# Preparation of an adaLN block on one core: four buffers of normalised tokens, modulation rows as two lines spread by transfers, values of nine tiles ahead of the scores

## The chip, the cores and the metric

The kernel runs on one core of a Trainium2 chip. The metric is the device time of one execution in microseconds (us); a kernel is given by the median of its runs.

## The reference

Two batches of 2048 tokens of width 256. Six modulation vectors come from `silu(c) @ wmod`. Then

```python
h = layernorm(x) * (1 + ca) + sa
q, k, v = h @ Wq, h @ Wk, h @ Wv            # 16 heads, key width 16, value width 64
attn = softmax(q k / 4, over the query axis)
x = x + ga * (attn @ v) @ Wo
h = layernorm(x) * (1 + cb) + sb
x = x + gb * ffn(h)     # gate, up (704 wide) and down, all with blockwise FP4 quantisation
```

`ga` and `gb` are pushed away from zero: `(2 * (g >= 0) - 1) * max(|g|, 0.25)`. All is float32.

## The kernel before

The program is written out by hand: five functions, one for each engine (`tensor_program`, `scalar_program`, `vector_program`, `gpsimd_program`, `sync_program`), each a fixed order of instructions, joined by semaphores. In the text PE is TensorE, DVE is VectorE, ACT is ScalarE, POOL is GpSimd, SP is SyncE, whose queue issues nearly all transfers. A float32 product is made of three products of 'high' and 'low' parts (`products`, L397), so most operands stand in two tensors, `*_hi` and `*_lo`.

For each batch `b` there is a preparation and then an attention loop; after both batches follows the feed-forward part (32 token tiles).

**Preparation** (`prepare_pe`, `prepare_act`, `prepare_dve`, `prepare_pool`). The tokens are 16 tiles of 128, in four groups `g` of four tiles. For a group DVE takes mean and variance (`stats`, L849), POOL the inverse root (`inverse_root`, L1162), DVE normalises (`normalise`, L859) into the buffer `xn_r`, which holds two groups, PE transposes (`turn_tokens`, L403), ACT applies the modulation and writes `hT` and its high part (`take_tokens`, L678), DVE makes the low part (`low_tokens`, L870). Then PE makes queries and keys of the group in four pieces `r` of six matmuls each (`queries_keys`, L446), ACT and DVE write the two halves of each piece (`part_act`, L691; `part_dve`, L942) and SP stores them to DRAM (L354). PE waits for `tok_low` before each group. When all 16 pieces have landed, SP loads them for heads 0 and 1 as stacks `stq`, `stk` (`load_stack`, L297, 8 transfers a head); later heads are loaded during the loop.

Then come the values (`values`, L453): for each of `EARLY` tiles PE makes two halves of 512 columns, six matmuls each; ACT copies the first (L709), DVE the second (L955). The results stand in four PSUM quarters used in rotation; the table `bank_uses` says who used a quarter before, and `take_quarter` waits until that one was read. In batch 0 the modulation rows stand behind tile 3 (`mod_rows_pe`, L460; `mod_rows_dve`, L908): four uses `n`, two for each batch, each with a stationary operand of silu(c) repeated over 128 columns (`scb`), so that every partition gets the row; DVE turns them into `ga`, `sbr`, `cb1`, `gb`. DVE also quantises the gate-up weights (batch 0) or the down weights (batch 1) in 18 steps (`weight_step`, L874, lines L888 to L904), two behind each tile's copy; when they are done PE transposes the weights (`turn_gate_up`, L470; `turn_down`, L479) and the first scores follow.

**Attention loop** (`attend_*`). `JT` = 256 steps `j`, one for each head and key tile. A step has two halves: PE makes scores into one of three slots (L533), DVE takes the maximum (L988), ACT the exponent into a ring of eight in `e_sb` (L752), and PE multiplies with the values seven steps later (`LAG` = 7, `attend`, L562). The values of the tiles that are not early are made in the first steps, one tile a step.

Memory is shared by address: the token buffer `x_v`, `wm` (columns of `wmod`) and the raw weights `wgu_r` lie in `v_sb`, which the values later fill tile by tile (1024 columns a tile); `xn_r`, `hT`, the query and key pieces `part_r` and the raw down weights `wd_r` lie in the exponents' ring `e_sb`.

## Time and profile before

| | us |
|---|---|
| median of 3 runs | 1799.43 (1797.51 to 1804.31) |
| profiled execution, its own time | 1800.63 |
| span of the profile | 1799.3 |
| PE busy | 1701.9 (95%) |
| DVE busy | 1663.2 (92%) |
| ACT busy | 1369.1 (76%) |
| POOL busy | 503.7 (28%) |
| HBM traffic | 88.50 MB, 49 GB/s on average |

The span is the time from the first to the last record of the profiled execution; its own time is longer by 1.3 us, for what lies around it. Busy shares are averages over the preparation, the attention loops (about three quarters of the span) and the feed-forward part.

### The profile page before, as it was taken

The numbers are of one execution on the slowest core, as the hardware profiler recorded it, in microseconds if no ns is written. First come the engines' busy times: TensorE is split into PE (matmuls) and PEld (weight loads), VectorE is DVE, ScalarE is ACT, GpSimd is POOL, SyncE is SP. The second block draws the span as 40 slices with busy tenths as digits, with TensorE's granted clock in tenths as the row PEclk, the third lists the DMA queues.
The fourth block names the chain that finished last, engine by engine and source line by source line (L and its number), as shares of the span: only waits on it lengthen the run. The fifth ranks groups of instructions, "written<-read, shape, count | busy, mean of one in ns | idle before, by whom it ended". The sixth has DMA issues, their size and how long they took to land.

```text
span 1799.3 us, 38060 instructions
## 1 busy us (share of the span) xinstructions
PE 1701.9 (95%) x15122; PEld 816.6 (45%) x15122; DVE 1663.2 (92%) x2367; ACT 1369.1 (76%) x2552; POOL 503.7 (28%) x983
## 2 busy tenths in 40 slices
PE   6989999999999999899999999999999899999996
PEld 5653222222222322672222222322223488889996
DVE  5789999999999999669999999999999699999995
ACT  4269999999999999549999999999999422222232
POOL 1101222122221222002122212221222446666664
PEclk9999999999999999999999999999999999999998
DMA  5201111100111102301100111101112212222200
GB/s 196 80 3 31 31 39 39 44 30 31 37 38 45 31 31 60 122 36 40 44 30 31 36 39 42 35 31 34 39 37 58 96 62 71 71 71 74 71 13 18
DMA packets 52434, 88.50 MB, mean 49 GB/s; under 512 B 3232, under 2 KB 34848, under 8 KB 52256
## 3 DMA queue, kind: packets, MB, share of 16 engines
q1 hardware_dynamic: 51840, 85.54, 14.6%
q8 instruction: 119, 1.95, 0.5%
q10 hardware_dynamic: 416, 0.53, 0.1%
q14 instruction: 59, 0.48, 0.1%
HBM read 56.69 MB, written 29.36 MB: 48 GB/s over the span
## 4 chain that ended last, share of the span: by engine, by line
PE 53%; ACT 22%; issue 14%; DVE 10%; POOL 2%; DVEq 0%; POOLq 0%; ACTq 0%
PE acc L562 25%; ACT e_sb L752 20%; PE slot L533 8%; PE slot L400 7%; PE acc L400 6%; PE acc L582 4%; DVE nm L988 1%; PE slot L623 1%; POOL hqT_lo L841 1%; DVE e_sb L1074 1%; DVE ost L999 1%; DVE e_sb L1070 1%; DVE e_sb L1075 1%; PE slot L416 1%; POOL v_sb L1173 0%
## 5 line engine op out<-in xcount | busy, mean ns | idle before, releaser
L988 DVE TENSOR_REDUCE nm<-slot 128x1 f32<-128x1024 f32 x1024 | 1181.0, 1220 | 10.6 <-PE slot L533 10.6
L752 ACT ACTIVATE e_sb<-slot,nm 128x1024 f32<-128x1024 f32 x1024 | 1140.1, 1113 | 26.8 <-DVE nm L988 25.7
L562 PE MATMUL acc<-e_sb,vp 64*64 64x512 f32 x8192 | 1068.1, 595 | 39.2 <-ACT ost L772 38.6
L533 PE MATMUL slot<-stq,stk 64*64 64x512 f16 x4096 | 418.2, 393 | 8.3 <-ACT e_sb L752 8.3
L533 PEld LDWEIGHTS slot<-stq,stk 64*64 64x64 f16 x4096 | 118.5, 104 | 671.6 <-ACT e_sb L752 633.0
L562 PEld LDWEIGHTS acc<-e_sb,vp 64*64 64x64 f32 x8192 | 283.7, 133 | 192.6 <-issue 92.6
L1226 POOL TENSOR_TENSOR dlt<-nm 128x4 f32<-128x4 f32 x128 | 25.4, 198 | 702.4 <-DVE nm L988 702.4
L752 ACT ACTIVATION_READ_ACCUMULATOR e_sb<-slot,nm 128x1 f32 x1024 | 197.3, 193 | 0.0
L1217 POOL TENSOR_TENSOR vp<-v_sb,fac 128x512 f32<-128x512 f32 x128 | 133.4, 1042 | 10.4 <-POOL fac L1207 0.7
L841 POOL TENSOR_TENSOR hqT_lo<-e_sb,hqT_hi 128x640 fp32r<-128x640 f32 x64 | 121.0, 1910 | 50.0 <-ACT hqT_hi L676 50.0
L795 ACT COPY e_sb<-slot 128x256 f32<-128x256 f32 x32 | 11.9, 373 | 159.3 <-PE slot L593 159.3
L1200 POOL TENSOR_TENSOR wsum<-cor,ssum 128x8 f32<-128x8 f32 x128 | 25.9, 203 | 272.6 <-ACT cor L780 272.6
L805 ACT COPY e_sb<-slot 128x640 f32<-128x640 f32 x32 | 22.3, 697 | 96.8 <-PE slot L623 96.8
L400 PE MATMUL slot<-wgu_hi,xqT_hi 128*128 128x352 f32 x256 | 85.9, 336 | 3.1 <-POOL xqT_lo L841 3.1
L400 PE MATMUL slot<-wgu_lo,xqT_hi 128*128 128x352 f32 x256 | 83.2, 325 | 0.0
L400 PE MATMUL slot<-wgu_hi,xqT_lo 128*128 128x352 f32 x256 | 83.1, 325 | 0.0
L400 PE MATMUL acc<-wdb_hi,hqT_hi 128*128 128x256 f32 x192 | 62.7, 326 | 16.3 <-POOL hqT_lo L841 9.1
L582 PE MATMUL acc<-v_sb 128*128 128x256 f32 x256 | 58.1, 380 | 1.9 <-DVE e_sb L1043 1.0
L582 PE MATMUL acc<-e_sb,v_sb 128*128 128x256 f32 x256 | 57.9, 379 | 0.0
L400 PE MATMUL acc<-wdb_lo,hqT_hi 128*128 128x256 f32 x192 | 56.3, 293 | 0.0
L400 PE MATMUL acc<-wdb_hi,hqT_lo 128*128 128x256 f32 x192 | 56.1, 292 | 0.0
L582 PEld LDWEIGHTS acc<-v_sb 128*128 128x128 f32 x256 | 48.0, 190 | 9.4 <-DVE e_sb L1043 1.8
(178 smaller groups left out, 1772.5 us busy)
## 6 DMA issues: line engine op xcount, KB each, us to landing
stk<-qk_parts SPq DMA_DIRECT2D x128, 128.0 KB
o_heads<-ost SPq DMA_DIRECT2D x64, 256.0 KB, 3.4
v_sb<-o_heads SPq DMA_DIRECT2D x8, 2048.0 KB, 8.6
v_sb<-in_x SPq DMA_DIRECT2D x16, 512.0 KB, 7.4
qk_parts<-e_sb SPq DMA_DIRECT2D x32, 256.0 KB, 2.2
stq<-qk_parts SPq DMA_DIRECT2D x128, 64.0 KB
out<-e_sb SPq DMA_DIRECT2D x32, 128.0 KB, 1.7
v_sb<-in_wgu SPq DMA_DIRECT2D x1, 1408.0 KB, 14.4
```

The source lines that it names most:

```text
L400: mm = pe.matmul(o, a, w, start=(n == 0 and m == 0), stop=(n == len(pairs) - 1 and m == 2))
L416: mm = pe.transpose(z[:, k * 512 + i * P:k * 512 + (i + 1) * P], xn_r[:, g % 2, i, k * P:(k + 1) * P], ident[:, :])
L533: mm = pe.matmul(slot[s][side * VD:(side + 1) * VD, c * 512:(c + 1) * 512], stk[c * 64:c * 64 + 64, h % 2, i * P + side * VD:i * P + (side ...
L562: mm = pe.matmul(acc[half * VD:(half + 1) * VD, c * 512:(c + 1) * 512], vp[rows, g % 3, gi, half, :], e_v[rows, j % ERING, n0:n0 + 512], s ...
L582: mm = pe.matmul(acc[:, 0:D], o_r[:, q % 2, c, r * P:(r + 1) * P], wob[b][:, c, :], start=(c == 0), stop=(c == 7))
L752: act.activation(e_v[:, j % ERING, half * 1024:(half + 1) * 1024], slot[u % 3][:, :], ACT.Exp, bias=nm[:, g % 4, i, half:half + 1], accum_ ...
L805: act.copy(hqT[:, i % 2, 0:5].rearrange("p a b -> p (a b)"), tp[:, 0:640])
L841: return eng.tensor_tensor(dst, full, hi.bitcast(F32), ALU.subtract)
L988: dve.tensor_reduce(nm[:, g % 4, i, half:half + 1], slot[u % 3][:, :], AX.X, ALU.max, negate=True).then_inc(maxed.sem)
L1200: pool.tensor_tensor(wsum[:, s], cor[:, s], ssum[:, s], ALU.mult).then_inc(sem)
L1217: pool.tensor_tensor(vp[:, g % 3], v_v[:, i0:i0 + GROUP, h * VD:(h + 1) * VD].unsqueeze(2).to_broadcast([P, GROUP, 2, VD]), fac[:, s].unsq ...
L1226: pool.tensor_tensor(dlt[:, s, :, 0], nm[:, s, :, 1], nm[:, s, :, 0], ALU.subtract)
```

## The change

- `xn_r`, and the small tensors of the statistics, hold four groups and not two. Where the other tenants of `e_sb` and `v_sb` lie changes with it. In batch 0 DVE does the statistics of group 3 and the normalising of groups 2 and 3 inside group 0. In batch 1 all four groups are done in the tail of batch 0's attention loop (step `JT + 2`).
- The high part of the value weights (`wv_hi`) is made by ACT in group 0, not group 2, so POOL's `wv_lo` can follow it.
- The modulation rows are made once for both batches, as two lines (two partitions, one for each batch): two uses and not four, with silu(c) itself as the stationary operand. DVE works on two partitions. SP stores the lines to DRAM behind the loads of the first two stacks, and loads them spread over all 128 partitions at step 16 of batch 0. ACT and DVE wait for that store (`rows_out`) before they copy values of tile 9, which lies over the lines. `scb` is gone.
- `EARLY` is 9 and not 12: three more tiles of values are made in the loop's first steps.
- Batch 0's weight steps start in group 3, one behind each piece.
- At the start POOL takes group 0's inverse root before the squares of the weights.

Cut to its core:

```diff
-EARLY = 12
+EARLY = 9
-        early += [("rows", n) for n in range(4)] if b == 0 else []
+        early += [("rows", n) for n in range(2)] if b == 0 else []
...
-        xn_r = region(e_sb, 0, 2, GROUP, D)
+        xn_r = region(e_sb, 0, NG, GROUP, D)
...
+                if b == 0:
+                    sp.wait_ge(*rows_made.past(1))
+                    sp.dma_start(rows_d.rearrange("v b d -> b v d"), mrow[0:B, :, :]).then_inc(rows_out.sem, 16)
                 for j in range(JT + LAG):
+                    if j == NT and b == 0:
+                        sp.wait_ge(*rows_out.past(0))
+                        for v, t in enumerate((ga, sbr, cb1, gb)):
+                            sp.dma_start(t[:, :, :], rows_d[v:v + 1].to_broadcast([P, B, D])).then_inc(got_rows.sem, 16)
...
-            for n in range(4):
-                m, c = divmod(n, 2)
+            for n in range(2):
                 o = take_quarter(0, "rows", n)
                 for k in range(2):
-                    mm = pe.matmul(o, scb[:, k, m, :], wm[:, k, 512 + c * 512:1024 + c * 512],
+                    mm = pe.matmul(o[0:B, :], sc4[:, 1, k, :], wm[:, k, 512 + n * 512:1024 + n * 512],
...
             if b == 0 and i == 4:
-                act.wait_ge(*rows_mm.past(3))
-                act.wait_ge(*rows_made.past(3))
+                act.wait_ge(*rows_mm.past(1))
+            if b == 0 and i == EARLY:
+                act.wait_ge(*rows_out.past(0))
...
-                if b == 0 and g == 2:
+                if b == 0 and g == 0:
                     act.wait_ge(*got_wv.past(0))
                     high(wv_hi[:, :, :], wv_s[:, :, :]).then_inc(wv_high.sem)
...
+                stats(0, 2)
+            step = 0
             for g in range(NG):
-                if g + 2 < NG:
-                    stats(b, g + 2)
                 for r in range(4):
                     part_dve(b, g, r)
                     if b == 0 and g == 0 and r == 1:
+                        normalise(0, 2)
+                        stats(0, 3)
                         low_tokens(0, 1)
-                    if g + 2 < NG and r == 1:
-                        normalise(b, g + 2)
+                        normalise(0, 3)
+                    if b == 0 and g == NG - 1:
+                        weight_step(b, step)
+                        step += 1
...
-                for s in range(2 * i, min(2 * i + 2, 18)):
+                for s in range(step, min(step + 2, 18)):
                     weight_step(b, s)
+                step += 2
...
                 if j == JT + 2 and b + 1 < B:
-                    stats(b + 1, 0)
-                    stats(b + 1, 1)
-                    normalise(b + 1, 0)
-                    normalise(b + 1, 1)
+                    for g in range(0, NG, 2):
+                        stats(b + 1, g)
+                        stats(b + 1, g + 1)
+                        normalise(b + 1, g)
+                        normalise(b + 1, g + 1)
```

How it moves instructions, in two places. First DVE, in batch 0's preparation, from the second piece of group 0 on (L945, and L952 in the new file, is `part_dve`; L852, L855, L857 and L862, L865, L867 are `stats`; L866 and L874 `normalise`; L841 and L851 with `hT_lo` are `low_tokens`, the number at its end is the group plus 58). Before:

```order
L945 SCALAR_TENSOR_TENSOR e_sb<-slot,even,e_sb 128x512 x2
L841 TENSOR_TENSOR hT_lo_59<-e_sb,hT_hi_63 128x1024
L866 TENSOR_SCALAR e_sb<-v_sb,mv,rstd 128x256 x4
L945 SCALAR_TENSOR_TENSOR e_sb<-acc,even,e_sb 128x512 x2
L841 TENSOR_TENSOR hT_lo_60<-e_sb,hT_hi_64 128x1024
L852 BN_STATS st<-v_sb 128x6 x4
L855 BN_AGGR mv<-st 128x2 x4
L857 TENSOR_SCALAR ve<-mv 128x4
L945 SCALAR_TENSOR_TENSOR e_sb<-slot,even,e_sb 128x512 x2
L866 TENSOR_SCALAR e_sb<-v_sb,mv,rstd 128x256 x4
L945 SCALAR_TENSOR_TENSOR e_sb<-acc,even,e_sb 128x512 x2
L841 TENSOR_TENSOR hT_lo_61<-e_sb,hT_hi_65 128x1024
```

and now:

```order
L952 SCALAR_TENSOR_TENSOR e_sb<-slot,even,e_sb 128x512 x2
L874 TENSOR_SCALAR e_sb<-v_sb,mv,rstd 128x256 x4
L862 BN_STATS st<-v_sb 128x6 x4
L865 BN_AGGR mv<-st 128x2 x4
L867 TENSOR_SCALAR ve<-mv 128x4
L851 TENSOR_TENSOR hT_lo_59<-e_sb,hT_hi_63 128x1024
L874 TENSOR_SCALAR e_sb<-v_sb,mv,rstd 128x256 x4
L952 SCALAR_TENSOR_TENSOR e_sb<-acc,even,e_sb 128x512 x2
L851 TENSOR_TENSOR hT_lo_60<-e_sb,hT_hi_64 128x1024
```

The normalising of group 2 now stands ahead of the low part of group 1, and that of group 3 directly behind it, where before it followed two pieces of group 1.

Second SP, in batch 0 (L308 and L310 are `load_stack`, L365 stores the two lines, L370 loads them spread, L317 stores a head). Around the store of the lines:

```order
L308 DMA stq<-qk_parts 32x2x512
L310 DMA stk<-qk_parts 32x1x2048
L365 DMA mod_rows<-v_sb 2x4x256
L308 DMA stq<-qk_parts 32x2x512
L310 DMA stk<-qk_parts 32x1x2048
```

and around the four loads:

```order
L308 DMA stq<-qk_parts 32x2x512
L310 DMA stk<-qk_parts 32x1x2048
L370 DMA ga<-mod_rows 128x512
L370 DMA sbr<-mod_rows 128x512
L370 DMA cb<-mod_rows 128x512
L370 DMA gb<-mod_rows 128x512
L317 DMA o_heads<-ost 64x1024 x2
```

The store stands behind all sixteen transfers of heads 0 and 1 and ahead of the eight of head 2; the loads stand behind those eight. The other rows of SP stand as before, without these five.

## Rows read from the trace of the kernel before

**Rows 1.** Windows: length, busy PE PEld DVE ACT POOL (x), PEclk, DMA share, GB/s

```profile
126.00:690.00 564.00, 545.98 (x5736) 166.35 (x5728) 558.36 (x612) 556.37 (x1030) 118.19 (x358) 1.00 0.11 34
```

**Rows 2.** Timeline, batch 0's start: start, length, engine, line, what [idle before <-releaser]

```profile
7.25 3.58 PE L646 MATMUL slot<-sc,v_sb 128*128 128x2 f32 x16 [7.25 <-DMA v_sb<-in_wmod]
12.24 1.97 PE L416 MATMUL slot<-ident,e_sb 128*128 128x128 f32 x8 [1.42 <-DVE e_sb L866]
14.36 1.45 ACT L687 ACTIVATE e_sb<-slot,sa,a 128x512 f32<-128x512 f32 x2 [5.53 <-DVE a L1134]
```

**Rows 3.** Timeline of PE: where it stands idle in the two preparations

```profile
30.18 1.70 PE L416 MATMUL slot<-ident,e_sb 128*128 128x128 f32 x8 [2.65 <-DVE e_sb L866]
...
40.56 1.84 PE L416 MATMUL slot<-ident,e_sb 128*128 128x128 f32 x8 [2.13 <-DVE e_sb L866]
...
57.04 0.50 PE L400 MATMUL slot<-wv_hi,hT_hi 128*128 128x512 f32 x1 [2.66 <-POOL wv_lo L841]
...
736.87 1.09 PE L416 MATMUL slot<-ident,e_sb 128*128 128x128 f32 x8 [1.05 <-DVE e_sb L866]
```

**Rows 4.** DVE's terms: a piece, the statistics and normalising; then its low parts, grouped

```profile
24.64 0.75 DVE L945 SCALAR_TENSOR_TENSOR e_sb<-slot,even,e_sb 128x512 f16<-128x512 f32 x1 [0.19 <-ACT e_sb L698]
...
717.21 1.37 DVE L852 BATCH_NORM_STATS2 st<-v_sb 128x6 f32<-128x256 f32 x4
...
721.04 2.84 DVE L866 TENSOR_SCALAR e_sb<-v_sb,mv,rstd 128x256 f32<-128x256 f32 x8
...
L841 DVE TENSOR_TENSOR hT_lo<-e_sb,hT_hi 128x1024 fp32r<-128x1024 f32 x4 | 4.9, 1225 | 10.2 <-ACT hT_hi L687 10.2
```

**Rows 5.** Timeline of POOL: low part of the value weights

```profile
51.42 5.56 POOL L841 TENSOR_TENSOR wv_lo<-wv_s,wv_hi 128x256 fp32r<-128x256 f32 x8 [12.44 <-ACT wv_hi L676]
```

**Rows 6.** Timeline of batch 0: modulation rows on DVE and PE, weight steps

```profile
71.57 0.42 DVE L914 COPY sbr<-slot 128x256 f32<-128x256 f32 x1 [0.95 <-PE slot L466]
...
79.71 1.63 DVE L900 TENSOR_TENSOR ost<-ost,vp 128x1408 f32<-128x1408 f32 x1
...
85.17 1.61 DVE L888 TENSOR_REDUCE qs<-v_sb 128x88 f32<-128x1408 f32 x1
...
98.56 0.69 DVE L955 COPY v_sb<-acc 128x512 f32<-128x512 f32 x1
...
73.08 3.60 PE L466 MATMUL acc<-v_sb 128*128 128x512 f32 x8
```

**Rows 7.** Timeline of PE: scores at steps 0, 4 and 9; step 0 of batch 1

```profile
103.29 0.41 PE L533 MATMUL slot<-stq,stk 64*64 64x512 f16 x4
...
118.70 0.63 PE L533 MATMUL slot<-stq,stk 64*64 64x512 f16 x8
...
132.94 0.40 PE L533 MATMUL slot<-stq,stk 64*64 64x512 f16 x4
...
794.37 0.41 PE L533 MATMUL slot<-stq,stk 64*64 64x512 f16 x4
```

**Rows 8.** Timeline of PE, batch 1: first values, first turned down weights

```profile
760.28 0.40 PE L400 MATMUL slot<-wv_hi,hT_hi 128*128 128x512 f32 x1
...
792.97 0.82 PE L486 MATMUL slot<-ident,e_sb 128*128 128x128 f32 x6
```

**Rows 9.** Stack loads: DVE's last piece, SP's first load, two windows, a store's landing

```profile
55.13 0.75 DVE L945 SCALAR_TENSOR_TENSOR e_sb<-acc,even,e_sb 128x512 f16<-128x512 f32 x1 [0.64 <-ACT e_sb L698]
...
58.16 0.80 SPq L307 DMA_DIRECT2D stq<-qk_parts  x1
...
60.50:91.50 31.00, 29.95 (x115) 21.49 (x114) 27.61 (x41) 4.70 (x8) 0.00 (x0) 0.99 0.13 51
...
91.00:92.00 1.00, 1.00 (x7) 0.81 (x5) 0.96 (x2) 0.20 (x1) 0.00 (x0) 1.00 0.07 29
...
qk_parts<-e_sb SPq DMA_DIRECT2D x32, 256.0 KB, 2.2
```

**Rows 10.** Windows, columns as in group 1: PE's clock behind its idle time

```profile
57.80:61.30 3.50, 3.50 (x10) 2.68 (x10) 0.00 (x0) 0.59 (x1) 0.00 (x0) 0.51 0.05 15
```

More of the change, by code:

```diff
@@ L908, in mod_rows_dve @@
         def mod_rows_dve():
-            for n in range(4):
-                m, c = divmod(n, 2)
-                o = quarter_of(0, "rows", n)
+            for n in range(2):
+                o = quarter_of(0, "rows", n)[0:B]
                 dve.wait_ge(*rows_mm.past(n))
-                if c == 0:
-                    dve.tensor_copy(sbr[:, m, :], o[:, 256:512])
-                    src, gate = o[:, 0:256], ga[:, m, :]
-                else:
-                    dve.tensor_scalar(cb1[:, m, :], o[:, 0:256], 1.0, None, ALU.add)
-                    src, gate = o[:, 256:512], gb[:, m, :]
-                sign, size = tmp[:, 0, c, :], tmp[:, 1, c, :]
+                if n == 0:
+                    dve.tensor_copy(mrow[0:B, 1, :], o[:, 256:512])
+                    src, gate = o[:, 0:256], mrow[0:B, 0, :]
+                else:
+                    dve.tensor_scalar(mrow[0:B, 2, :], o[:, 0:256], 1.0, None, ALU.add)
+                    src, gate = o[:, 256:512], mrow[0:B, 3, :]
+                sign, size = tmp[0:B, 0, :], tmp[0:B, 1, :]
                 settle(dve.tensor_scalar(sign, src, 0.0, 2.0, ALU.is_ge, ALU.mult))
@@ L952, in take_values_dve @@
                 dve.wait_ge(*normalised(b, NG - 1))
-            if b == 0 and i == EARLY + 1:
+            if b == 0 and i == EARLY:
+                dve.wait_ge(*rows_out.past(0))
+            if b == 0 and i == 13:
                 dve.wait_ge(*gu_turn.past(5))
+            if b and i == 10:
+                dve.wait_ge(*dn_turn.past(3))
             dve.tensor_copy(v_sb[:, i * HV + 512:(i + 1) * HV], quarter_of(b, "v", 2 * tile + 1)).then_inc(v_dve.sem)
@@ L1183, in prepare_pool @@
                 pool.tensor_tensor(bound[:, 1], bound[:, 0], quarter4[:, :, :], ALU.pow).then_inc(root_made.sem)
-            for g in range(2, NG):
-                inverse_root(b, g)
-            if b == 0:
+                for g in range(2, NG):
+                    inverse_root(b, g)
                 pool.wait_ge(*wv_high.past(0))
@@ L1228, in attend_pool @@
                 if j == JT + 2 and b + 1 < B:
-                    inverse_root(b + 1, 0)
-                    inverse_root(b + 1, 1)
+                    for g in range(NG):
+                        inverse_root(b + 1, g)
                 if j == JT + 2 and b == B - 1:
```

53 lines of the change are left out of this document (27 added, 26 removed).

## The prediction

> **What bounds the kernel now.** I read the windows by stage first. In an attention loop [rows 1] DVE and ACT are busy 99% of the time and PE 97%, and the change edits nothing inside it but the first steps. So the gain has to come from the two preparations, where I read PE's timeline for the places at which it stands idle, and who ends that: in batch 0 a late normalise on DVE, twice, and then POOL's `wv_lo`; in batch 1 a normalise again [rows 3]. Third I read what stands on DVE there [rows 4, 6], and last the transfers that run beside the values [rows 9]. All sums are made against the profiled execution: span 1799.3, its own time 1800.63; the median shown is 1799.43, 1.2 lower. A measurement here can tell about 0.5% (9 us) from no change.
>
> **Start of batch 0.** PE's first product ends at 7.25 + 3.58 = 10.83 and the first transposes start at 12.24, waiting for a normalise; ACT takes the result 0.15 behind their end [rows 2]. The inverse root now stands ahead of POOL's squares, so the normalise is ready before 10.83, and the transposes follow at once: 1.4 earlier. I take the x groups as landed in time. Bounds: 0 (x is late) and 1.4.
>
> **Groups in batch 0.** Group 0's keys end at 30.18 - 2.65 = 27.53 [rows 3], now 26.1. Group 2's normalise is ready (it starts behind DVE's second piece, which ends at 24.64 + 0.75 - 1.4 = 24.0 [rows 4]), so its transposes run at once, 0.9 us. Group 1's matmuls wait for its low part: on DVE stand 24.0, then normalise 1.42, statistics 1.91 (the two groups between 717.21 and 721.04 halved), low part 1.22 [rows 4], so 28.5. That is 1.2 later than it could be, but 3 earlier than before. A group is 24 matmuls, 5.6 us at full clock. Then nothing is late: 28.5 + 5.6, transposes 0.9, and two groups without a gap (ACT and DVE need 2.8 + 1.2 behind the transposes, under 5.6), end at 46.2. Before it was 57.04 - 2.66 = 54.38 [rows 3]. `wv_lo` takes 5.56 [rows 5] and starts at about 32, where ACT's cast now stands, so it is done by 38 and the values start at 46.2, 10.8 earlier.
>
> **From there DVE is the bound.** Its work from group 3's first piece (at 42.7: PE's first piece, 1.4, and ACT's half, 0.7, behind 40.6) to the last weight step is: 4 pieces, 2.8; all 18 weight steps; 7 copies at 0.61; the modulation rows. Nine steps are 98.56 - 85.17 less four copies = 10.95 [rows 6], so 21.9. The rows were four uses in 79.71 - 71.57 = 8.1 [rows 6], two are now 4.1 if two partitions cost what 128 do. The lower bound is near 0.8 for ten fixed costs, the upper 4.1; I take the upper. Sum 33.1, so 75.8. PE itself needs 9 tiles at 2.72 and four matmuls, half of 2 x 3.6 [rows 6], 3.3 less overlap: 46.2 + 24.5 + 3.3 = 74.0, so it waits 1.8 us. The turned gate-up weights take 2.6 (22 transposes, by the 1.40 for 12 in batch 1 [rows 7, 8]), and the scores start at 78.4 instead of 103.29: **-24.9**.
>
> **The first steps of the loop.** With values a step takes (118.70 - 103.29)/4 = 3.85 [rows 7]; there are seven such steps now and not four, so step 7 starts 26.95 behind step 0. From there steps go at the loop's pace, 564 us for 245 of them, 2.3 each [rows 1]. Before, 29.65 led to step 9's second half [rows 7]; now it is 26.95 + 5 halves at 1.15 = 32.7. **+3.0** for each batch. (Three tiles cost 8.2 us ahead of the scores. Part of what is saved is that PE no longer idles in steps 4 to 6.)
>
> **The new wait.** ACT and DVE wait for `rows_out` ahead of tile 9's copies, which stand in step 0, and PE needs the quarter for tile 10 at step 0 + 4.2, so at 82.6. The store is issued behind both stacks. Before, those loads began 2.3 us behind DVE's last piece (55.88, 58.16), ran at 51 GB/s with 0.13 of the engines busy, which is two of sixteen, and traffic stopped at 91.5 [rows 9], 33.3 us later. Now DVE's last piece ends at 42.7 + 2.8 + three small steps 2.6 = 48.1, so traffic stops at 83.7. If the store of two lines, one on each of two partitions, queues behind it, it lands at about 85.5 (a store needs 2.2 in all [rows 9]), ACT's copy is done at 86.1 and PE stands 3.5 us. After 2.13 to 2.66 us of idle time PE's clock fell to the lower of its two levels, 1.2 GHz, for some 3.5 us [rows 3, 10]: another 1.8. Together **+5.3**. The other bound is 0: the store goes by other engines and lands 2.2 behind its issue, at about 74.5. The deciding row is the 0.13: a transfer with an outer dimension of two keeps to two engines, and the store has one too. I take 5.3. The Trainium skill ("DMA: Bandwidth & Descriptors", "Why a DMA increments its semaphore by 16 and not by 1") says that a transfer uses the largest number of engines up to 16 that divides both slowest dimensions, the lowest-numbered ones; by this rule the store shares the stacks' two engines, which speaks against this part of the change. The rows agree for the stacks; none shows the store. The four spread loads at step 16 are read only by the fold and the feed-forward part, hundreds of us later; I cost them at nothing.
>
> PE's wait of 1.8 us ahead of the gate-up weights lies between 1.05, after which the clock held, and 2.13, after which it fell [rows 3]; half of 1.8 is **+0.9**.
>
> Batch 0: -24.9 + 3.0 + 5.3 + 0.9 = **-15.7**.
>
> **Batch 1.** In the tail DVE does four groups, two rounds of 6.67 (717.21 to 723.88 [rows 4]), until 730.5, then group 0's low part until 731.7. Group 0's matmuls began near 730.1 (they end at 736.87 - 1.05 [rows 3]), so they start 1.6 later. PE's own attends go on meanwhile. Then nothing is late: 4 x 5.6 + 2 x 0.87 gives 755.8 for the first value, before 760.28 [rows 8], -4.5. Nine tiles at 2.72 end at 780.3. DVE's last two weight steps stand behind the ninth copy now: copy 0.6, steps 0.9 each (half as wide as in [rows 6]), so PE idles until 782.7, turns the weights in 1.40, and the scores start at 784.1, before 794.37 [rows 7]: **-10.3**. Steps +3.0, less about 0.5, because before PE's clock fell there as well; and the clock behind 2.4 us of idle time +1.8. **-6.0**.
>
> Sum -21.7: span 1777.6, own time 1778.9, as a median **1777.7**.
>
> **The rivals.** (1) *The store is not behind the stacks, or lands in time.* It stands for it that it is 8 KB. Against it stands the two-engine queue. -5.3: 1772.4. (2) *Preparation stays tighter than I think*: PE's clock falls in group 1 behind its 1.2 us wait too (1.8 more, passed on to DVE's chain), an order of waits between ACT and DVE costs 1 to 2 in each batch, and the front gives 0. In sum 6 to 9: about 1785. (3) *The wait takes all.* `rows_out` holds ACT and DVE in step 0, one for one from 82.6 on. Without it the sum is -27.0. To end more than 9 us slower than before the store would have to land at 118 or later, that is, the stacks' 33 us would double; it takes a second flow on the two engines, and no row shows one at that time. 1812. (4) *The change does not do what it says*: the early normalises are not what frees PE, since the low part behind ACT's four passes ends last; then groups 1 to 3 keep their gaps, about -7 is lost together with half of the values' gain in DVE-bound stretches, 1792.
>
> **How the numbers follow.** The forecast has 0.52, rival 1 0.22, rival 2 0.17, rival 4 0.06, rival 3 0.03. Around the forecast the bounds are -3 (rows on two partitions are cheap, clock holds) and +5. Range 1769 to 1787: it takes in rival 1 with its own -3 and rival 2. Faster by over 0.5% means under 1790.4: the first three, and a part of the fourth, 0.93. Within: 0.04. Slower: 0.03.
>
> **What would show it.** Right: PE has no idle time of over 1.5 us between 27 and 75 us; first values near 46; first scores of batch 0 near 78 and of batch 1 near 784; a wait of 3 to 4 us on a transfer at ACT's or DVE's copy of tile 9, with a lower clock behind it; a wait near 2 us of PE for the last weight step in both batches; a loop whose heads take what they took. Wrong: first scores of batch 0 behind 84, a gap between groups 2 and 3, or heads that take longer from end to end. Had the copy of tile 9 no wait, rival 1 holds.

## The result, and the profile after

The changed kernel takes 1777.24 us (median of 4 runs, 1775.41 to 1780.47), the kernel before beside it 1799.65 (1797.51 to 1804.31): ratio 0.9874, 95% interval 0.9849 to 0.9899. It is faster by 22 us, 1.3%. The prediction was 1777.7, range 1769 to 1787. The profiled execution took 1776.08, its span is 1774.8 (1799.3 before), so the two profiles differ by 24.5.

The profile's page: span, busy times and the chain of waits by line. The chain now holds a transfer, the store of the modulation lines, that no row of before has.

```profile
span 1774.8 us, 38040 instructions
...
PE 1687.0 (95%) x15114; PEld 805.4 (45%) x15114; DVE 1663.4 (94%) x2356; ACT 1368.5 (77%) x2552; POOL 500.3 (28%) x983
...
PE acc L569 25%; ACT e_sb L760 20%; PE slot L540 8%; PE acc L408 7%; PE slot L408 6%; PE acc L589 4%; DVE e_sb L1092 1%; DVE nm L1004 1%; SPq L310 1%; PE slot L630 1%; DVE e_sb L1091 1%; DVE e_sb L1087 1%; DMA mod_rows<-v_sb 1%; DVE ost L1015 1%; DVE st L862 1%
```

The timeline of PE in the two preparations of after: every place at which it is idle for over 1 us once it has started, with the modulation rows and batch 1's first values between them. (Columns as in the rows ahead of the prediction: start, length, engine, line, what, idle before and who ended it.)

```profile
28.34 0.50 PE L408 MATMUL slot<-hT_hi,wq_hi 128*128 128x512 f32 x1 [1.94 <-DVE hT_lo L851]
...
57.14 3.60 PE L473 MATMUL slot<-v_sb,sc 128*2 128x512 f32 x8
...
75.85 1.26 PE L483 MATMUL slot<-ident,v_sb 128*128 128x128 f32 x8 [1.29 <-DVE v_sb L912]
...
85.81 0.80 PE L408 MATMUL acc<-wv_hi,hT_hi 128*128 128x512 f32 x1 [2.98 <-ACT v_sb L717]
...
714.94 0.50 PE L408 MATMUL slot<-hT_hi,wq_hi 128*128 128x512 f32 x1 [1.61 <-DVE hT_lo L851]
...
738.98 0.39 PE L408 MATMUL slot<-wv_hi,hT_hi 128*128 128x512 f32 x1
...
766.22 0.88 PE L493 MATMUL acc<-ident,v_sb 128*128 128x128 f32 x6 [2.58 <-DVE v_sb L912]
```

The three idle times of [rows 3] in batch 0 are gone, and so are those for a normalise in batch 1. Before had two of these there: the 1.05 us of [rows 3], and a longer one that [rows 3] leaves out, behind which PE's clock fell (0.60 from 746.6 to 750.1):

```profile
746.63 1.37 PE L416 MATMUL slot<-ident,e_sb 128*128 128x128 f32 x8 [3.12 <-DVE e_sb L866]
```

In their place PE waits for low parts (1.94, 1.61), for DVE's last weight step (1.29, 2.58), and at 85.81 for ACT, which itself waited for a transfer. Five marks cut the program into stages in all kernels: the first scores of each batch, the first and the last copy of a finished head to `ost` on DVE, and the end. These are their rows in after (the scores of before are [rows 7]):

```profile
78.57 0.41 PE L540 MATMUL slot<-stq,stk 64*64 64x512 f16 x4
...
767.68 0.41 PE L540 MATMUL slot<-stq,stk 64*64 64x512 f16 x4
```

```profile
147.13 0.69 DVE L1015 COPY ost<-acc 128x512 f32<-128x512 f32 x1 [0.31 <-PE acc L569]
...
1395.78 0.69 DVE L1015 COPY ost<-acc 128x512 f32<-128x512 f32 x1 [2.60 <-PE acc L569]
```

and the two copies in before:

```profile
163.81 0.69 DVE L999 COPY ost<-acc 128x512 f32<-128x512 f32 x1 [0.31 <-PE acc L562]
...
1419.74 0.69 DVE L999 COPY ost<-acc 128x512 f32<-128x512 f32 x1 [2.60 <-PE acc L562]
```

From the same marks of all profiles comes this table (us; "first steps" runs from the first scores to the first head's copy, and the like; the median is that of the timed runs; after was timed and profiled twice):

| kernel | first scores | first steps | to scores of batch 1 | to last copy | rest | span | median |
|---|---|---|---|---|---|---|---|
| before | 103.29 | 60.52 | 630.56 | 625.37 | 379.56 | 1799.3 | 1799.65 |
| after | 78.57 | 68.56 | 620.55 | 628.10 | 379.02 | 1774.8 | 1777.24 |
| after, again | 78.50 | 68.29 | 620.63 | 628.19 | 377.49 | 1773.1 | 1776.82 |
| store between stacks | 78.98 | 64.24 | 621.10 | 629.20 | 380.98 | 1774.5 | 1772.43 |
| store on ACT's queue | 79.12 | 64.15 | 620.60 | 628.06 | 379.67 | 1771.6 | 1772.60 |
| rows in four uses | 83.24 | 64.47 | 620.64 | 629.63 | 378.92 | 1776.9 | 1778.14 |
| values of twelve tiles | 85.99 | 61.22 | 625.99 | 624.63 | 382.27 | 1780.1 | 1781.31 |
| late normalises | 88.05 | 69.92 | 626.13 | 629.53 | 379.07 | 1792.7 | 1790.92 |
| low part first | 79.79 | 68.59 | 620.52 | 627.96 | 378.14 | 1775.0 | 1776.71 |
| squares late | 78.17 | 68.23 | 620.47 | 627.94 | 380.69 | 1775.5 | 1777.25 |
| weight steps of batch 1 early | 78.42 | 68.52 | 617.71 | 628.05 | 379.60 | 1772.3 | 1773.10 |
| five moves | 77.27 | 64.24 | 617.82 | 628.16 | 380.61 | 1768.1 | 1767.55 |
| five, without group 2's steps | 77.51 | 64.14 | 617.82 | 628.16 | 383.47 | 1771.1 | 1770.96 |
| five moves and the tail | 77.63 | 64.15 | 616.09 | 628.11 | 379.12 | 1765.1 | 1766.41 |

Of the 24.5 us of after, 24.7 are won ahead of the first scores, 8.0 lost in the first steps, 10.0 won up to the scores of batch 1, 2.7 lost behind them, 0.5 won in the rest. Note the column "rest": no kernel changes anything there, and it goes from 377.49 to 383.47. The last section shows that the granted clock of PE differs there from run to run. So an effect of 1 to 5 us is read here from the marks ahead of it, not from the end.

### The profile page after: what moved, and what is told of

Its sections match the earlier page's. It is cut to its first block, busy times and chain, and to the rows that moved or that the text cites. A ratio compares the mean times of both kernels' runs of the same rounds, so it can differ in the third digit from the quotient of the medians.

```text
span 1774.8 us, 38040 instructions
## 1 busy us (share of the span) xinstructions
PE 1687.0 (95%) x15114; PEld 805.4 (45%) x15114; DVE 1663.4 (94%) x2356; ACT 1368.5 (77%) x2552; POOL 500.3 (28%) x983
## 4 chain that ended last, share of the span: by engine, by line
PE 51%; ACT 21%; issue 13%; DVE 11%; POOL 2%; SPq 1%; DMA 1%; DVEq 0%; POOLq 0%; ACTq 0%
PE acc L569 25%; ACT e_sb L760 20%; PE slot L540 8%; PE acc L408 7%; PE slot L408 6%; PE acc L589 4%; DVE e_sb L1092 1%; DVE nm L1004 1%; SPq L310 1%; PE slot L630 1%; DVE e_sb L1091 1%; DVE e_sb L1087 1%; DMA mod_rows<-v_sb 1%; DVE ost L1015 1%; DVE st L862 1%
## 5 line engine op out<-in xcount | busy, mean ns | idle before, releaser
L851 POOL TENSOR_TENSOR hqT_lo<-e_sb,hqT_hi 128x640 fp32r<-128x640 f32 x64 | 115.8, 1829 | 50.3 <-ACT hqT_hi L683 50.3
L1267 POOL TENSOR_TENSOR e_sb<-e_sb,qs 128x704 f32<-128x704 f32 x32 | 45.5, 1423 | 30.2 <-DVE e_sb L1126 30.2
```

The costliest lines, as they stand in the source:

```text
L851: return eng.tensor_tensor(dst, full, hi.bitcast(F32), ALU.subtract)
L1267: pool.tensor_tensor(blocks(hq[:, i % 3, :]), blocks(xn_h[:, i % 2, :]), wide(qs[:, 1, (i % 2) * 44:(i % 2) * 44 + 44], 44), ALU.mult).the ...
```

## The experiments

All are made from the changed kernel, and each is compared with it stage by stage.

**1. The store of the lines between the two stacks.**

```diff
                 load_stack(b, 0)
-                load_stack(b, 1)
                 if b == 0:
                     sp.wait_ge(*rows_made.past(1))
                     sp.dma_start(rows_d.rearrange("v b d -> b v d"), mrow[0:B, :, :]).then_inc(rows_out.sem, 16)
+                load_stack(b, 1)
```

> The changed kernel with the store of the two modulation lines issued between the stacks of head 0 and head 1, not behind both. Theory (the store stands behind the stacks in SP's queue): head 0's loads carry half of the traffic that stopped at 83.7 us, so the store lands near 70, ACT and DVE find no wait ahead of tile 9's copies, PE's clock holds, and step 3 of batch 0 (88.67 us in the profile of after) starts near 84.4; the span falls by 4.3 to about 1770.5. Rival A (the wait stands in the place of another one in the first steps, the exponentials above all): the transfer's wait goes, but the span falls by under 1. Rival B (a store from two partitions is slow by itself): it lands over 8 us behind its issue and the wait stays at 2 us or more.

First the stall as after shows it. SP's queue, with the store behind the last stack load; the windows around its landing (columns as in [rows 1]); and the copies of tile 9:

```profile
71.42 1.90 SPq L310 DMA_DIRECT2D stk<-qk_parts  x1
73.37 2.13 SPq L365 DMA_DIRECT2D mod_rows<-v_sb  x1
```

```profile
83.00:84.00 1.00, 0.00 (x0) 0.00 (x0) 0.00 (x0) 0.00 (x0) 0.00 (x0) 1.00 0.13 53
84.00:85.00 1.00, 0.00 (x0) 0.00 (x0) 0.00 (x0) 0.00 (x0) 0.00 (x0) 1.00 0.03 12
85.00:86.00 1.00, 0.19 (x1) 0.20 (x2) 0.82 (x2) 0.83 (x2) 0.00 (x0) 0.75 0.00 0
```

```profile
85.17 0.59 ACT L717 COPY v_sb<-acc 128x512 f32<-128x512 f32 x1 [3.60 <-DMA mod_rows<-v_sb]
```

```profile
85.18 0.69 DVE L966 COPY v_sb<-acc 128x512 f32<-128x512 f32 x1 [3.01 <-DMA mod_rows<-v_sb]
```

```profile
85.80:89.30 3.50, 3.49 (x11) 2.17 (x12) 1.27 (x3) 2.79 (x5) 0.00 (x0) 0.55 0.02 5
```

The store is issued at 73.37 and lands 11.8 us later, when the stacks' traffic at 0.13 of the engines has ended; from 83 to 85 every engine of the core is idle. PE stands 2.98, and in the 3.5 us behind that its granted clock is 0.55 of full speed on average, so nearly all of that time is spent at the lower of its two levels. With the store between the stacks, SP's queue and the copies of tile 9 read:

```profile
64.97 0.26 SPq L364 DMA_DIRECT2D mod_rows<-v_sb  x1
```

```profile
81.89 0.58 ACT L717 COPY v_sb<-acc 128x512 f32<-128x512 f32 x1
```

```profile
82.95 0.69 DVE L966 COPY v_sb<-acc 128x512 f32<-128x512 f32 x1 [0.35 <-PE acc L408]
```

The transfer's wait is gone, and step 3's scores start at 84.77 (expected 84.4). The first steps take 64.24 instead of 68.56: **4.3 us, as expected**, and rivals A and B fall. The profile's span is only 0.3 lower, because PE's clock fell ahead of batch 1's scores (0.63 from 762.38 to 765.88; the two columns of batch 1 are 1.7 longer in sum) and the rest took 2.0 more. The median, 1772.43, is 4.8 under that of after.

**2. The same store on ACT's queue.**

```diff
             for i in range(EARLY):
+                if b == 0 and i == 6:
+                    act.wait_ge(*rows_made.past(1))
+                    act.dma_start(rows_d.rearrange("v b d -> b v d"), mrow[0:B, :, :]).then_inc(rows_out.sem, 16)
                 take_values_act(b, i)
```

(and SP's own store left out)

> The same store at its old date, as soon as the lines are made (64.6 us), while both stacks are under way, but issued on ACT's queue ahead of tile 6's copy. If what held it is the order inside SP's queue alone: it lands 2 to 4 us behind its issue, near 68, and the span falls by 4.3 as with the store between the stacks. If it is the two engines, full until 83.7 whichever queue a transfer comes from: it lands near 84 and the span is unchanged (1774.8). Between the two (the engines take turns between queues): landing between 70 and 80 and a gain of 3 to 4.3.

ACT's queue, a window of DMA traffic late in the stacks, and the copy of tile 9:

```profile
65.65 0.50 ACTq L737 DMA_DIRECT2D mod_rows<-v_sb  x1
```

```profile
83.00:84.00 1.00, 1.00 (x8) 0.68 (x8) 0.92 (x2) 0.97 (x2) 0.00 (x0) 1.00 0.12 49
```

```profile
82.03 0.58 ACT L714 COPY v_sb<-acc 128x512 f32<-128x512 f32 x1
```

The stacks' traffic runs on, at 0.12 beyond 83, but the store was home before 82.03: no wait, first steps 64.15, 4.4 saved. That alone doesn't tell which of two things helped, another queue or an issue 7.7 us earlier: with the 11.8 us of after a store issued at 65.65 would have landed at 77.4, in time too. The packets of the transfers decide it. In this kernel the queue q10 has ten packets more than in after, and q1, the queue of the stacks, ten fewer, so q10 is ACT's. All ten run between 69.00 and 69.40 (packets of all queues in these 0.4 us, then by queue: packets, MB, share of 16 engines):

```profile
DMA packets 20, 0.02 MB, mean 46 GB/s; under 512 B 2, under 2 KB 20, under 8 KB 20
...
q1 hardware_dynamic: 10, 0.01, 7.2%
q10 hardware_dynamic: 10, 0.01, 6.0%
```

They are eight of 1 KB and two of 4 bytes; every stack transfer ends in two packets of 4 bytes as well. (In after the store's ten are the last of q1, from 83.86 to 84.64.) At 69.4 eight stack transfers had ended, while eleven had been issued in full on SP's queue ahead of 65.65. So the store passed three that were issued before it, and was through 3.7 us behind its issue, with the stacks' traffic going on beside it. What held the store in after was neither the traffic as such nor its late issue, but that it stood behind the stacks in the same queue. Of the three landings expected, "2 to 4 us behind its issue, near 68" came nearest. The Trainium skill ("DMA: Bandwidth & Descriptors", "Queues, rings and completion order") says that SP and ACT each have a ring of their own on every engine and that an engine takes turns between the rings it has work for; this run agrees, with ten packets of each queue in those 0.4 us. (A ring is a queue of one transfer engine.)

**3. The modulation rows in four uses, written straight to their tables.** This undoes the part of the change that makes two lines and spreads them by transfers.

```diff
-            for n in range(2):
+            for n in range(4):
+                m, c = divmod(n, 2)
...
-                    mm = pe.matmul(o[0:B, :], sc4[:, 1, k, :], wm[:, k, 512 + n * 512:1024 + n * 512],
+                    mm = pe.matmul(o, scb[:, k, m, :], wm[:, k, 512 + c * 512:1024 + c * 512],
...
-            if b == 0 and i == EARLY:
-                dve.wait_ge(*rows_out.past(0))
```

> The changed kernel with the modulation rows as before: four uses of a quarter, each of 128 partitions, written straight into their tables, no store and no spread loads. Theory: DVE's chain to the last weight step gets 4.1 longer (8.1 against 3.97), so the scores of batch 0 start near 82.7 and not at 78.57; the wait for the store goes (4.3 back); the span is within 1 of 1774.8. So this part of the change brought nothing as it stands. Rival (the lines spread by transfers are a gain): PE's four longer products (7.2 against 3.6) count in full beside DVE's, the scores start at 84 or later, and the span is 1776.5 to 1779.

The same operation of DVE on the rows, on 2 partitions in after and on 128 in this kernel:

```profile
61.37 0.41 DVE L928 SCALAR_TENSOR_TENSOR v_sb<-v_sb,slot 2x256 f32<-2x256 f32 x1
```

```profile
61.89 0.42 DVE L922 SCALAR_TENSOR_TENSOR v_sb<-v_sb,slot 128x256 f32<-128x256 f32 x1
```

Two partitions cost what 128 cost, so only the halved number of operations saves: 8.1 us against 4.0. The scores start 4.7 later (4.1 expected: the work on the rows is 4.15 longer, and it begins 0.5 later, as PE's first product, which waits for a transfer, began 0.6 later in this run), and the first steps give 4.1 back. At the first head's copy the kernel is 0.6 behind after. The span is 2.1 higher, beyond the 1 that was expected; 1.6 of it came in batch 1, where the clock fell. **The two lines were worth 4 us ahead of the scores, and their store took the 4 us back.**

**4. Twelve tiles of values ahead of the scores.**

```diff
-EARLY = 9
+EARLY = 12
...
-        mrow = region(v_sb, 9216, 4, D)
-        tmp = region(v_sb, 10240, 2, D)
+        mrow = region(v_sb, 12288, 4, D)
+        tmp = region(v_sb, 7552, 2, D)
```

> The changed kernel with twelve tiles of values ahead of the scores again, and all the rest as changed (the lines' buffer moved to tile 12's place, so that the wait for their store stands at tile 12's copy, again in step 0). Theory: in batch 0 PE, no longer DVE, is the bound of the values, the scores start 6.5 later (85.1), the store has landed by then (4.3 back), and four steps and not seven carry values (3.0 back): -0.8. In batch 1 the 2.6 us for which PE waited on the last weight step are filled: 8.2 - 2.6 - 3.0 = +2.6. Span +1.8, near 1776.6. Rival (nine tiles are worth what they take off the front, less what the steps give back): +5.2 in each batch, 1785.

Batch 0: scores 7.4 later, first steps 7.3 shorter, together +0.1 (expected -0.8). Batch 1: +5.4 and -3.5, +2.0 (expected +2.6; the wait for the last weight step is filled). At the last copy +2.05 in all, near the +1.8 expected, and far from the rival's 10. Against experiment 1, which has no stall either, twelve tiles cost 7.0 - 3.0 = 4.0 in batch 0. In batch 1, against experiment 8, which has no 2.58 us wait, they cost 4.9. So nine tiles are worth 4 to 5 us to a batch when nothing else stands in the way, and in the kernel as changed the stall of batch 0 and the 2.58 us wait of batch 1 ate 4 and 3 of it. PE's clock has a hand in this: with twelve tiles it falls in the first steps of each batch (here, and at 0.50 from 792.6 to 799.4; in before at 122.7 and 815.6), with nine it fell only behind the stall.

```profile
106.50:113.30 6.80, 5.53 (x40) 1.73 (x40) 5.33 (x5) 6.11 (x11) 1.34 (x3) 0.50 0.01 2
```

How much the clock makes of the 4 us no run tells apart. The median is 4.1 above that of after, of which the marks explain 2; the profiled run was 3.2 longer in the rest, where the code is the same; its granted clock was 0.97 on average there and 0.98 in after.

**5. Normalises of groups 2 and 3 at their old dates, four buffers kept.**

```diff
-                        normalise(0, 2)
-                        stats(0, 3)
                         low_tokens(0, 1)
-                        normalise(0, 3)
+                    if g + 2 < NG and r == 1:
+                        normalise(b, g + 2)
```

(and in the tail of batch 0 groups 0 and 1 alone)

> The changed kernel with statistics and normalises of groups 2 and 3 at their dates of before, in both batches (four buffers are kept, but groups 2 and 3 are normalised only behind the second piece of groups 0 and 1, and in the tail of batch 0 only groups 0 and 1). Theory: PE waits for the normalises of groups 2 and 3 again, 2.1 to 2.7 us each time with its clock falling behind it; in batch 0 the values start near 53.2 (54.38 of before less the 1.17 gained at the start) and not at 46.2, in batch 1 4.5 later (743.6 against 739.1, without what is passed on from batch 0); everything behind moves by as much, DVE's weight steps and the stacks with their store too. Span +11.6, near 1786.4. Rival (the low part behind ACT's four passes ends last, not the normalise): no gap and under 2 us.

PE, DVE and POOL in this kernel:

```profile
29.19 1.51 PE L424 MATMUL slot<-ident,e_sb 128*128 128x128 f32 x8 [2.64 <-DVE e_sb L874]
...
40.88 1.97 PE L424 MATMUL slot<-ident,e_sb 128*128 128x128 f32 x8 [3.47 <-DVE e_sb L874]
...
55.65 0.39 PE L408 MATMUL slot<-wv_hi,hT_hi 128*128 128x512 f32 x1
```

```profile
37.94 2.88 DVE L874 TENSOR_SCALAR e_sb<-v_sb,mv,rstd 128x256 f32<-128x256 f32 x4
```

```profile
37.77 5.71 POOL L851 TENSOR_TENSOR wv_lo<-wv_s,wv_hi 128x256 fp32r<-128x256 f32 x8
```

The gaps for the normalises are back at once, so the rival (the low part ends last) falls; that was rival 4 of the prediction. The cost is 17.9 and not 11.6. Of the difference, 2.4 is ahead of the values (55.65 against 53.2): the second normalise took 2.88 us instead of 1.38, because `wv_lo`, which the change moved forward, now runs on POOL beside it, and behind PE's longer idle time (3.47) the clock stayed at the lower level for 6.8 us (0.50 from 40.0 to 46.8), where in before it was back at 44.1. The rest is spread: 1.4 in the first steps, and in batch 1 5.6 + 1.4 against 4.5, the clock's fall behind the 2.58 us wait in it. **The early normalises are the largest part of the gain: 14 us by the medians, 18 by the profiles.**

**6. Group 1's low part ahead of group 3's statistics.**

```diff
                         normalise(0, 2)
-                        stats(0, 3)
                         low_tokens(0, 1)
+                        stats(0, 3)
                         normalise(0, 3)
```

> The changed kernel with the low part of group 1 ahead of the statistics of group 3 on DVE. In the profile of after PE waited 1.94 us for it (until 28.34) although ACT's result for it was there near 25.5. Theory: the low part ends at 26.8, group 1's products start 1.6 earlier, and as DVE's chain to the last weight step hangs on group 3's pieces, the scores of batch 0 start 1.6 earlier; but the stall on the store of the lines stays (the stacks and the store hang on the same pieces): span -1.6, 1773.2. Rival: group 3's normalise, now 1.2 later, or wv_lo becomes the late one: a gap ahead of group 3's transposes or of the first values, and no gain.

PE and DVE behind the swap:

```profile
27.45 0.49 PE L408 MATMUL slot<-hT_hi,wq_hi 128*128 128x512 f32 x1 [0.49 <-DVE hT_lo L851]
...
32.55 0.50 PE L408 MATMUL acc<-hT_hi,wk_hi 128*128 128x512 f32 x1 [2.05 <-DVE e_sb L952]
```

```profile
30.45 1.38 DVE L874 TENSOR_SCALAR e_sb<-v_sb,mv,rstd 128x256 f32<-128x256 f32 x4 [1.12 <-POOL rstd L1182]
31.75 1.40 DVE L952 SCALAR_TENSOR_TENSOR e_sb<-acc,even,e_sb 128x512 f16<-128x512 f32 x2
```

A miss: 1.2 later, not 1.6 earlier. Group 1 starts 0.9 earlier, but then DVE waits 1.12 for POOL's inverse root ahead of the normalise, and behind that stand group 0's last two pieces, for whose quarters PE then waits 2.05 us. The rival's direction was right, its place was not: neither group 3's transposes nor `wv_lo`, but the pieces. In after the low part stands in the gap that the inverse root leaves (DVE still waits 0.9 behind it).

**7. POOL's squares behind the first normalise.**

```diff
             pool.wait_ge(*got_qkw.past(0))
+            pool.wait_ge(*normalised(0, 0))
             pool.tensor_tensor(wsq[0], wq_s[:, :, :], wq_s[:, :, :], ALU.mult)
```

> The changed kernel with POOL's two squares of the weights started behind DVE's first normalise and not beside it. In the profile of after this normalise took 2.81 us (four of 128x256) beside the squares, every other one 1.38. Theory (the two engines hold each other up while both read and write SBUF): it takes 1.4 again and ends near 9.6, so the first transposes follow PE's first product at once, 0.64 earlier, and the squares take about 1.0 each as they did; the squares end near 11.7, still ahead of DVE's low parts of the weights (13.5). Span -0.6. Rival (it is slow because it is the first use of this operation on the DVE, or because its x is just landing): it takes 2.8 again and ends as before, and nothing moves.

After first: DVE's first normalise, its first operation alone, and POOL's squares; then the normalise in this kernel.

```profile
8.21 2.81 DVE L874 TENSOR_SCALAR e_sb<-v_sb,mv,rstd 128x256 f32<-128x256 f32 x4 [1.15 <-POOL rstd L1182]
```

```profile
8.21 1.12 DVE L874 TENSOR_SCALAR e_sb<-v_sb,mv,rstd 128x256 f32<-128x256 f32 x1 [1.15 <-POOL rstd L1182]
```

```profile
8.15 1.04 POOL L1279 TENSOR_TENSOR e_sb<-wq_s 128x512 f32<-128x512 f32 x1
9.14 1.09 POOL L1280 TENSOR_TENSOR e_sb<-wk_s 128x512 f32<-128x512 f32 x1
```

```profile
8.16 1.38 DVE L874 TENSOR_SCALAR e_sb<-v_sb,mv,rstd 128x256 f32<-128x256 f32 x4 [1.15 <-POOL rstd L1182]
```

The normalise takes 1.38 again, so it was the squares. In after its first two operations last 1.12 each, as the two squares do (1.04 and 1.09), and the other two 0.40, as all four in this kernel (0.41): each of the first two waits for a whole instruction of POOL. The first scores are 0.4 earlier, though PE's first product ended 0.5 later in this run, and the last copy is 1.0 earlier (1394.81); the expected 0.6 lies between. The median, 1777.25, shows nothing of it.

**8. Batch 1's weight steps from group 3 on.**

```diff
-                    if b == 0 and g == NG - 1:
+                    if g == NG - 1:
                         weight_step(b, step)
                         step += 1
```

> The changed kernel with batch 1's weight steps begun in group 3, one behind each piece, as in batch 0, not with the first values. Theory: DVE's last weight step no longer stands behind the ninth copy, PE's idle time of 2.58 us ahead of the turned down weights goes, the scores of batch 1 start 2.6 earlier, the clock can't fall there (it held at 1.00 in the profile of after, but was at 0.55 behind the same wait in two of four other profiles, 1.6 us): span -2.6 against a run whose clock held, -4.2 against one whose clock fell; the median some 3 lower. Rival (the weights' load, issued when batch 0 is attended, or group 3's pieces are held up by the steps): the values of batch 1 start later by what is gained, span unchanged.

The stage to the scores of batch 1 is 2.84 shorter (620.55 to 617.71), PE has no idle time ahead of the down weights, and the median is 4.1 lower. (The expectation speaks of two of four profiles and of 0.55; it was two of the three others that had this wait then, at 0.63 and 0.70 in the 3.5 us behind it.) The rival falls.

**9 to 11. What the findings give together**, beside the changed kernel once more. Five moves: those of experiments 1, 7 and 8; the low part first with group 3's normalise behind the fourth piece; two weight steps in group 2 of batch 0.

```diff
                         normalise(0, 2)
-                        stats(0, 3)
                         low_tokens(0, 1)
+                        stats(0, 3)
+                    if b == 0 and g == 0 and r == 3:
                         normalise(0, 3)
-                    if b == 0 and g == NG - 1:
+                    if g == NG - 1 or b == 0 and g == NG - 2 and r % 2:
                         weight_step(b, step)
```

> The changed kernel with five moves together: the store of the lines between the two stacks; POOL's squares behind the first normalise; group 1's low part ahead of group 3's statistics, and group 3's normalise behind the fourth piece of group 0 (so that no piece stands behind an inverse root); batch 1's weight steps from group 3 on; two of batch 0's weight steps in group 2. Theory, from the single runs against after: store -4.3, squares -0.6, steps of batch 1 -3.9, group 1's products 0.9 earlier, and PE's wait of 1.3 ahead of the gate-up weights gone: -11.0, span 1763.8, median near 1766. Rival (the front gains are taken up by PE, which is the bound as soon as DVE is not): squares, low part and the steps in group 2 give 1 and not 2.8, 1765.6. Rival (the steps in group 2 hold up the pieces, PE waits in group 3): the scores of batch 0 start at 78 or later, 1767.

> The same without the two weight steps in group 2. Theory: DVE's last weight step is again what PE waits for ahead of batch 0's gate-up weights, by 1.3 or more, and the scores of batch 0 start 1.3 to 2.4 later than with them: span 1765.1 to 1766.2. Rival (DVE's chain has no room in group 2, the two steps only move the wait): no difference.

> The changed kernel itself once more, for the comparison on the same chip: median 1777 within 1.5, its profiled wait for the store of the lines again near 3 us; its first normalise again 2.8 us; whether the clock falls behind the 2.58 us wait of batch 1 is open.

To the last copy the five moves save 8.3 us (1387.49 against 1395.78), not 11: 4.3 in the first steps and 2.7 in batch 1 as measured alone, but only 1.3 ahead of the scores. The first rival is right. The two steps in group 2 bring next to nothing (0.14 up to the last copy, against the 1.3 to 2.4 expected, so their rival holds): without them PE waits 1.28 for the last weight step, with them twice for DVE's copies of values, 0.96 in sum. The medians, 1767.55 and 1770.96, differ by more, but in the profiles that lies in the rest, and the one timed run without the steps that had the highest granted clock (0.996, the others 0.993 and 0.994) took 1767.35, against 1767.31 to 1769.39 for the runs with them (0.995 and 0.996). The changed kernel came out at 1776.82, with waits of 2.56 for the store's copy and 2.58 for the weights, and a first normalise of which one operation took 1.12.

**12. The tail too.**

```diff
                         stats(b + 1, g + 1)
-                        normalise(b + 1, g)
-                        normalise(b + 1, g + 1)
+                        if g == 0:
+                            normalise(b + 1, g)
+                            normalise(b + 1, g + 1)
...
                     low_tokens(b + 1, j - JT - 5)
+                if j == JT + 5 and b + 1 < B:
+                    normalise(b + 1, 2)
+                    normalise(b + 1, 3)
```

> The five moves together, and in the tail of batch 0 the normalises of groups 2 and 3 behind group 0's low part and not ahead of it. In the profile of the five moves PE waits 1.61 us for that low part (until 709.39), whose other input, ACT's, is ready near 704. Theory: the low part starts 2.8 earlier, PE goes from its last attends into group 0's products without the wait, and the scores of batch 1 start 1.6 earlier; span 1.6 under that of the five moves at an equal clock in the feed-forward part (last copy of a head 1385.9 and not 1387.5), median near 1766. Rival (the normalises are now late for group 2's transposes, or push group 0's pieces back): PE waits there instead, no gain.

The stage to batch 1's scores is 1.73 shorter (616.09), with no idle time of PE over 0.8 us in either preparation. At the last copy it is 1.5 ahead of the five moves (1385.98; 1385.9 expected), so the rival falls. Its median is 1766.41 us (1764.65 to 1769.01), ratio to before 0.9813, 95% interval 0.9798 to 0.9829. The changed kernel beside the five moves had 0.9884 (0.9863 to 0.9904), so the six moves together are faster than it; the five moves had 0.9823 (0.9807 to 0.9840), and the times alone don't tell the sixth from none.

## Why the prediction was right, point by point

**Ahead of the scores, batch 0: -24.9, measured -24.7.** The steps held nearly one by one. ACT took the first tokens 1.17 earlier (13.19) and not 1.4: the transposes did not follow PE's first product at once (it ended at 10.44, they began at 11.08), because of the held-up normalise of experiment 7, which the working did not have. Group 1's matmuls from 28.34 (28.5), first values 46.16 (46.2), last weight step until 75.8 (75.8), scores 78.57 (78.4). The choice of the upper bound for the rows on two partitions, 4.1, was right (4.0). PE's wait for the last weight step was 1.29 and not 1.8, and the clock held behind it, so the term +0.9 did not occur. Three parts of the change were not run alone: the earlier high part of the value weights (PE's 2.66 us wait for `wv_lo` is gone), the inverse root ahead of the squares (the transposes begin 1.16 earlier) and batch 0's weight steps in group 3. For them the rows show that the waits went, and no run shows what each is worth.

**First steps: +3.0.** Nine against twelve tiles without a stall, experiments 1 and 4, gives 64.24 - 61.22 = 3.0 in batch 0, and 3.7 against before; in batch 1 it is 2.7 against before and 3.5 against experiment 4. The clock's fall in the first steps, which the working counted for batch 1 alone (0.5), was there in batch 0 of before as well (0.50 from 122.7 to 129.5), and is gone in both batches of experiment 1.

**The new wait: +5.3, measured 4.3.** Landing 85.17 (predicted 85.5). PE stood 2.98 and not 3.5, and the lower clock cost 1.3 rather than 1.8. The mechanism, a store behind the stacks, is shown by experiments 1 and 2, but the reason given for it was wrong in one point: the deciding row was said to be the two engines of sixteen. Experiment 2 has the same share of the engines busy, and the store passes three stack transfers issued before it. The queue decides. The rule on the number of engines in the Trainium skill ("DMA: Bandwidth & Descriptors", "Why a DMA increments its semaphore by 16 and not by 1") fits the 0.13 of the stacks, and the two packets of 4 bytes at the end of the store and of every stack transfer fit two engines for both, though no row names the engines; to share them was not enough for a wait. Rival 1, the store in time, was the right price for the right remedy: -4.3 instead of -5.3.

**Batch 0 as a whole: -15.7, measured -16.7** at the first head's copy. The clock's term (0.9) did not occur and the stall was 1.0 smaller; the first steps cost 0.7 more than +3.0, the front gave 0.2 less.

**Batch 1: -6.0, measured -7.3** (-10.0 and +2.7). The scores came 10.0 earlier (10.3 predicted), with PE idle for 2.58 (2.4). The term that failed is the clock behind that wait, +1.8: it held in after. Experiments 1, 3 and 5 show it falling behind the very same wait, in the first two for some 1.6 us, so the size was near and its occurrence a matter of the run: 3 of the 8 profiles with this wait.

**The sum:** -21.7 against -24.5 in the two profiles and -22.4 in the medians. The prediction's 1777.7 against 1777.24 is closer than its working deserves. The sum was 2.8 short of what the profiles show; but the profiled execution of after was 1.2 us under the median of its runs, and that of before 1.0 over its own, which took 2.1 of it back. That is luck, and so are the 0.5 us won in the rest, where nothing was changed: stage by stage the sum was 1.0 short in batch 0 and 1.3 in batch 1.

**The rivals.** Rival 4, that the normalises are not what frees PE, fell with experiment 5. Rival 2 had as its parts a fall of the clock in group 1, which did not come behind 1.94 us, and a smaller front gain, of which 0.2 came. Rival 3 needed a second flow behind which the store waits; the store landed at 85.17.

## What to carry to other kernels

A small transfer on which a compute engine waits belongs ahead of the bulk ones in its queue, or in another queue: 8 KB behind two stacks cost 4.3 us and undid what its producer had saved. When a front part of a program is shortened, list what is late next on each engine before believing the sum; here nine tiles and the two lines were worth some 4 us each in batch 0 only once the stall behind them was gone. An instruction that is moved on one engine must be laid beside what runs on its neighbour at that time, and an order on one engine that leaves a wait for another may be right because something useful stands in the gap (experiment 6).

## What the runs showed of the hardware that was not expected

**DVE and POOL hold each other up by whole instructions.** A normalise of four 128x256 operations takes 1.38 us alone, 2.81 beside POOL's two squares and 2.88 beside `wv_lo`; POOL's `wv_lo` took 6.59 us among DVE's work in after and 5.56 in [rows 5] (one of its eight operations took 1.72 beside a low part of DVE, the others 0.73 to 0.75), and its inverse root beside a low part on DVE 1.91, otherwise 1.01:

```profile
27.06 1.22 DVE L851 TENSOR_TENSOR hT_lo<-e_sb,hT_hi 128x1024 fp32r<-128x1024 f32 x1
```

```profile
27.23 1.91 POOL L1182 TENSOR_TENSOR rstd<-ve,mhalf 128x4 f32<-128x4 f32 x1 [3.52 <-DVE ve L867]
```

The Trainium skill ("SBUF — State Buffer", "SBUF: two separate sides") describes a pair of ports that the two engines share under an exclusive hold for a whole instruction. The rows agree: the first normalising operation of after ends at 9.33, just behind the square that ends at 9.19, and the inverse root ends 0.86 behind the low part that ends at 28.28. The effect held PE's first transposes up by 0.6 us in after (10.44 to 11.08) and DVE's normalise by 1.5 in experiment 5.

**The same wait, another clock.** Behind 2.58 us of PE's idle time ahead of the down weights, windows of 3.5 us show the granted clock at 1.00 in after, and at 0.69 with the rows in four uses (it fell in 3 of the 8 profiles that have this wait):

```profile
766.20:769.70 3.50, 3.48 (x26) 2.52 (x26) 1.23 (x1) 1.93 (x7) 0.00 (x0) 1.00 0.13 51
```

```profile
766.90:770.40 3.50, 3.50 (x20) 2.55 (x21) 1.22 (x1) 1.73 (x7) 0.00 (x0) 0.69 0.13 49
```

In before it fell behind 2.66 ([rows 3, 10]), and behind the 2.13 of [rows 3] too:

```profile
40.60:44.10 3.50, 3.50 (x13) 3.11 (x14) 1.22 (x2) 1.67 (x3) 0.00 (x0) 0.52 0.59 195
```

So the length of a wait alone does not tell whether the clock falls. The rest of the program, feed-forward included, shows the same. It took 377.49 us in one profile of the changed kernel and 383.47 in that of the five moves without group 2's steps (experiment 10). In the slower one the clock fell 17 us behind the last copy already, where the other kept it:

```profile
1404.80:1408.20 3.40, 3.40 (x13) 3.40 (x12) 3.30 (x7) 1.38 (x2) 0.15 (x1) 0.50 0.00 0
```

The last stretch of the two reads (granted clock 0.85 and 0.77)

```profile
1732.60:1773.10 40.50, 26.58 (x158) 23.68 (x156) 21.97 (x38) 8.58 (x20) 14.42 (x14) 0.85 0.05 17
```

```profile
1724.60:1771.10 46.50, 31.27 (x166) 27.59 (x166) 25.01 (x43) 9.21 (x22) 17.36 (x16) 0.77 0.06 18
```

Both stretches begin 337.0 us behind the last copy. The slower kernel has more left to do there (166 of PE's instructions against 158) and does it at a lower clock. The 6.0 us between them are a quarter of the change's effect, in code that no kernel here touches.
